# ScalarE's affine step of the image three ahead at step 54 instead of 48, the backward decayed sums two steps later

## The reference

```python
x = x + conv(_gn(x))          # a scale per image and channel from DCT sums of _gn(x)
t = _to_tokens(x)             # 16 x 1024 tokens of 128 channels
t = t + attn(_ln_t(t))        # 8 heads of 16: softmax attention, and a second branch
                              # attn2[i,j] = exp(-|i-j|/e), normalised, on t-values
t = t + ffn(_ln_t(t))         # the two best of 8 experts for each token
```

## Time and profile before

| what | us |
|---|---|
| median of 3 runs (2433.8, 2426.03, 2401.63) | 2426.03 |
| time of the profiled execution | 2445.75 |
| its span | 2443.8 |
| PE busy, share of the span | 2090.1, 86% |
| DVE busy | 1844.8, 75% |
| ACT busy | 1473.4, 60% |
| POOL busy | 1021.8, 42% |

### The profile page before, as it was taken

One profiled execution on the slowest core, in us unless ns is written; L12 is line 12 of the kernel. 1 busy time (PEld: TensorE's weight loads), 2 busy tenths in 40 slices (PEclk: granted clock), 3 DMA queues, 4 the chain that ended last, 5 costly groups with the idle time before them and its releaser, 6 DMA issues.

```text
span 2443.8 us, 34275 instructions
## 1 busy us (share of the span) xinstructions
PE 2090.1 (86%) x11456; PEld 921.0 (38%) x11456; DVE 1844.8 (75%) x2613; ACT 1473.4 (60%) x2913; POOL 1021.8 (42%) x1479
## 2 busy tenths in 40 slices
PE   2788999999999989999999999999999557777744
PEld 1333333333333333333333333333333146666633
DVE  5768789798979889897978889798981356666732
ACT  1137677677767777777767777677775223344420
POOL 2201233534343433534342443424133546677765
PEclk9999999899999999999999999899995578999975
DMA  5320222313132222213132222214011168666659
GB/s 170 60 39 14 40 49 41 94 31 76 27 75 44 46 48 42 59 31 82 28 68 45 45 51 39 62 27 80 10 54 68 43 208 285 221 207 197 210 165 343
DMA packets 100982, 215.00 MB, mean 88 GB/s; under 512 B 30224, under 2 KB 50392, under 8 KB 100376
## 3 DMA queue, kind: packets, MB, share of 16 engines
q1 hardware_dynamic: 78000, 166.96, 27.8%
q0 software_dynamic: 17280, 35.95, 4.2%
q10 hardware_dynamic: 5528, 9.91, 1.2%
HBM read 104.30 MB, written 61.23 MB: 68 GB/s over the span
## 4 chain that ended last, share of the span: by engine, by line
PE 55%; DVE 11%; POOL 10%; DMA 8%; issue 5%; SPq 5%; ACT 4%; ACTq 1%; POOLq 0%; DVEq 0%
PE ps L905 23%; PE ps L917 17%; POOL y_dram L783 8%; DVE row_max L1460 7%; SPq L541 4%; DMA region<-in_x 3%; ACT region L1208 3%; DMA region<-y_dram 2%; PE ps L881 2%; PE ps L859 2%; PE ps L867 2%; DMA big<-w_dram 2%; DMA y_dram<-region 2%; PE ps L936 1%; PE ps L871 1%
## 5 line engine op out<-in xcount | busy, mean ns | idle before, releaser
L1460 DVE TENSOR_REDUCE row_max<-ps 128x1 f32<-128x1024 f32 x1024 | 1236.7, 1216 | 250.6 <-PE ps L881 233.9
L1208 ACT ACTIVATE region<-ps 128x512 f32<-128x512 f32 x2048 | 1101.9, 600 | 396.2 <-PE ps L905 384.5
L905 PE MATMUL ps<-big 50*128 50x512 f32 x2048 | 852.3, 484 | 76.1 <-ACT region L1208 57.8
L881 PE MATMUL ps<-big 48*128 48x512 f32 x2048 | 852.6, 484 | 38.8 <-DVE row_max L1460 23.8
L905 PEld LDWEIGHTS ps<-big 50*128 50x128 f32 x2048 | 347.8, 194 | 799.5 <-ACT region L1208 376.4
L917 PE MATMUL ps<-region 128*32 128x512 f32 x4096 | 586.9, 647 | 0.0
L881 PEld LDWEIGHTS ps<-big 48*128 48x128 f32 x2048 | 347.8, 196 | 81.0 <-DVE row_max L1460 59.6
L783 POOL DMA_INDIRECT y_dram<-region x284 | 272.7, 960 | 125.3 <-issue 83.2
L729 POOL DMA_INDIRECT xs_dram<-region,slot x256 | 249.9, 976 | 81.1 <-issue 71.8
L665 POOL TENSOR_TENSOR norm_v<-norm 128x8 f32<-128x8 f32 x32 | 6.7, 211 | 658.8 <-DVE norm L1450 658.8
L1053 PE MATMUL ps<-big 128*128 128x512 f32 x284 | 126.9, 447 | 75.1 <-DMA big<-w_dram 74.3
(11 more groups left out here) (185 smaller groups left out, 1978.2 us busy)
## 6 DMA issues: line engine op xcount, KB each, us to landing
big<-w_dram SPq DMA_DIRECT2D x71, 514.0 KB, 4.6
big<-q_parts SPq DMA_DIRECT2D x384, 64.0 KB, 2.4
big<-k_parts SPq DMA_DIRECT2D x372, 64.0 KB, 2.4
region<-xs_dram SPq DMA_DIRECT2D x71, 264.0 KB, 2.9
region<-y_dram SPq DMA_DIRECT2D x16, 1024.0 KB, 10.0
region<-in_x SPq DMA_DIRECT2D x28, 512.0 KB, 5.2
t_dram<-region SPq DMA_DIRECT2D x16, 512.0 KB, 3.4
out<-region ACTq DMA_DIRECT2D x16, 512.0 KB, 6.1
```

What stands on the lines that cost most here:

```text
L881: mm = pe.matmul(ps[:, M_BANK + 2 * (n % 2) + c, :], lane_rows(q_stack[k % 2], h, SHIFT_ROW)[:, t * P:(t + 1) * P], lane_rows(k_stack[k % ...
L905: pe.matmul(ps[:, bank, :], lane_rows(k_stack[k % 2], h, STACK)[:, t * P:(t + 1) * P], lane_rows(q_stack[k % 2], h, STACK)[:, c * BANK:(c ...
L1208: act.activation(probs[:, u % 2, step_head(k, s, i), :], ps[:, bank, :], ACT.Exp, scale=DH ** -0.5).then_inc(exp_done, 1)
L1460: dve.tensor_reduce(row_max[:, h * TILES + t:h * TILES + t + 1], ps[:, at:at + 2, :], AX.XY, ALU.max).then_inc(max_done, 1)
```

## The change

Two constants. ScalarE's affine step goes from step 48 to step 54, so its wait for the load and its 128x1024 activation stand behind the exponentials of step 54. The eight pieces of the backward sums go from steps 28, 30, ..., 42 to 30, 32, ..., 44. The forward steps are written out and stay what they were. No instruction, transfer or wait is added or taken out.

```diff
-AT_FORWARD = tuple(range(8, 24, 2))
-AT_BACKWARD = tuple(range(28, 44, 2))
+AT_FORWARD = (8, 10, 12, 14, 16, 18, 20, 22)
+AT_BACKWARD = (30, 32, 34, 36, 38, 40, 42, 44)
...
-AT_AFFINE = 48
+AT_AFFINE = 54
```

## The result

The changed kernel takes 2349.23 us (median of 4 executions, 2341.54 to 2356.0), the kernel before 2422.06 us (4 executions, 2401.63 to 2433.8). The ratio is 0.9707 with a 95% interval of 0.9633 to 0.9781: **faster by 2.9%, 72.8 us between the medians.** Forecast were 2352 us and 74 us. The profiled execution took 2341.54 us, its span is 2339.6.

What follows compares the result with a forecast made beforehand. ScalarE's 12 waits for image loads, idling TensorE and lowering its clock, were taken to bound it: -85.3 + 4.8 + 3 = -77.5 us; with 74 us for the median, 2426 - 74 = 2352 us, range 2325 to 2390 us.

Steps and rivals of the forecast that it cites:

- What bounds it: Images 1 to 12, behind step 45: ScalarE's load waits idle TensorE and lower its clock; 109.93 us each against 102.82 undisturbed.
- Part 1: Affine step at 54: load there at least 5.4 us early, all 12 waits and the low clock go, gaining 85.3 us.
- The charge of 4.8 us for the affine step: ScalarE's 1.24 us of affine work, images 1 to 12: 0.4 us charged each, 4.8 us back (0 to 14.9).
- The charge of 3 us for the sums: Backward sums on VectorE, steps 30 to 44: 0.2 us per image in 15 images, 3 us (-2 to 11).
- the 0.13 us more: VectorE's scan at step 44: could take 0.13 us longer if GpSimd works beside it, 2 us over 15 images.
- net forecast of 77.5 us: Whole kernel, profiled execution: -85.3 + 4.8 + 3 = -77.5 us, from 2445.75 to 2368 us.
- GpSimd's queue: Step 49's slot computation, behind the later image addition: its wait of 7.57 us shrinks to 4.4, sends not later.
- The step to the median: Whole kernel: 74 us taken for the median in place of 77.5, as the profiled execution may have longer low-clock stretches.
- A: TensorE, images 1 to 12: the wait goes but the clock stays low; only 29.6 us gained, 2396 us; chance 0.07.
- B: Thin covers: affine step and both moves cost their upper bounds, 14.9 and 11 us; 2370 us; chance 0.17.
- C: Step 0 of the next image: stall moves to the image border, TensorE waits for shift rows; 2441 us; chance 0.03.
- D: Image load still comes after ScalarE in some images as its chain stretches; half the gain, 2389 us; chance 0.05.

Runs made afterwards that it cites:

- the run with the transposes: Kernel before, with 20 TensorE transposes added at step 48 in images 1 to 12, the wait for the load left in: 2395.64 us, one execution.
- the extra products: Changed kernel plus unused score-like TensorE products in image 15 from step 24 on, head order of the other images: 2336.81 us, ratio 0.963 to the kernel before.

## Why the prediction was right, step by step

**What bounds it:** right. Undisturbed images were put at 102.82 us from an image without an affine step; they take 102.6 to 103.1 us.

**Part 1, the wait and the clock: 85.3 us forecast.** The gross gain was right; undoing either cause alone shows both, an earlier load (82 us net with the affine step at 48) and a later step (86). The load lands 5.8 us early where at least 5.4 were said. Half of the loss was put down to the clock; the run with the transposes gives it at least 35 of 85 us.

**The charge of 4.8 us for the affine step: mis-sized.** At 54 it is nothing that can be seen: the two exponentials right behind it end 0.9 us later than in image 13 of the kernel before, which has no affine step, and the four after them end at the same point of the order. ScalarE had waited 0.87 us for TensorE there. My row for it, image 0, has the step at 48, where it costs 0.35 us indeed (the early load). I took a price from another place in the order.

**The charge of 3 us for the sums: mis-sized,** and with the wrong sign in the pair of traces with the affine step at 54: -0.6 us. The timed executions don't exclude 3 us, and while the wait is there they show 10 (4 to 17). In the trace the tail ahead of the scan at step 30 and the scan at 44 found room, as the slack of 0.43 us said for the latter. The scan at 44 takes 0.47 us in image 8, with no GpSimd operation beside it, so the 0.13 us more that were thought possible don't come. One small operation even became shorter, last section. The net forecast of 77.5 us became 86.5.

**GpSimd's queue:** right. The wait ahead of the slots in image 7 is

```profile
968.95 0.46 POOL L735 TENSOR_TENSOR picked<-pick,place 128x128 f32<-128x128 f32 x1 [4.83 <-DVEq L1583]
```

with 4 to 5 us forecast.

**The step to the median:** 3.5 us were taken off for chance in the profile. The two profiled executions show 86.5 us in the twelve images, the medians only 72.8 in all; the executions without a profile don't tell which part of them differs. Charges that were 9 us too high and a step to the median that was some 10 us too small nearly cancelled, so the median is right in part by luck.

**Rivals.** A (the clock stays low) fell: 1.00 over 1232 us. In the changed profile's image 14 the clock does fall for some 7 us, behind an idle time of only 0.83 us, and this stretch takes 101.13 us against 99.97. The Trainium skill's rule on short idle times (TensorE: Matmul & The Clock Gate, "A second HAM failure mode") would fit this, but the trace doesn't show it: the kernel before has the same 0.83 us at the same place of image 14 and keeps a clock of 1.00 over the whole stretch. What makes the clock fall behind so short a pause stays open; it was worth 1 us here. B fell: neither upper bound was met. C fell: even at 62 no image from 1 to 12 waits for its shift rows. D fell: no wait is left.

## What to carry to other kernels

A wait for a DMA on an engine with slack can be paid by the engine that it feeds: here TensorE paid it, and paid again while its clock was down. So look for the chain that brings the data, compare its length with where the taker stands in the order, and move the taker behind it (or the DMA ahead of the queue that delays it); a fraction of the wait removed is not the same fraction of the time; here TensorE's idle time was the measure that the loss followed. Take the price of a moved operation from its new surroundings.

## What wasn't expected of the hardware

**A tiny operation priced by its neighbour.** VectorE's subtraction of 128x8 values (L1559, two inputs in SBUF) took 0.46 us on average before and 0.17 after; the first row is the kernel before, the second the changed one:

```profile
L1559 DVE TENSOR_TENSOR gate_v<-gate_v 128x8 f32<-128x8 f32 x16 | 7.3, 459 | 0.1
```

```profile
L1559 DVE TENSOR_TENSOR gate_v<-gate_v 128x8 f32<-128x8 f32 x16 | 2.7, 166 | 0.1
```

It hadn't changed; GpSimd's addition (from 1111.97 in image 8) used to run beside it and now comes later. With the affine step alone moved it stays at 0.457; with the sums alone moved it takes 0.167. The Trainium skill (SBUF — State Buffer, on the shared port pair) says that a VectorE instruction with two SBUF inputs and a GpSimd one that reads SBUF keep each other out for a whole instruction. The trace agrees. Of the scans, which also have two SBUF inputs, 112 of 128 go from 529 ns on average to 505, and to 476 with the sums at 36 to 50, away from most of GpSimd's work. The other 16, the first of each image, go from 486 to 555 in the changed kernel and are back at 485 in that run.

**TensorE busy and the clock still at the lower level.** In image 15 of the kernel before, TensorE is busy for 61.18 of 64 us at 0.50:

```profile
1838.00:1902.00 64.00, 61.18 (x219) 23.14 (x211) 9.22 (x32) 31.18 (x58) 24.14 (x29) 0.50 0.22 79
```

With the extra products the clock in image 15's two stretches is 0.95 and 0.87, against at most 0.93 and 0.71 in the eleven profiles without them. It still isn't 1.00, and what would make it so isn't settled by these runs.
